# First attention's scores: six bf16 products of three parts replaced by three fp32r products of two 12-bit parts, two heads at a time

## The reference

```python
# 16 heads of 16 channels; l = 2048; b = 2
q, k, v = proj(q_w), proj(k_w), proj(v_w)                  # [b, h, l, 16]
scores = einsum('bhid,bhjd->bhij', q, k) / sqrt(16)
scores = scores - abs(j - i) * slope[h]                    # alibi
attn   = softmax(where(j <= i, scores, -inf), axis=-1)     # causal
out    = einsum('bhij,bhjd->bhid', attn, v) @ o_w
# then: layer norm, a spectral product (one folded 256x256 matrix), layer norm,
# a channel attention, layer norm, 8 experts of 1024 hidden units, layer norm
```

## Time and profile before

| | |
|---|---|
| median of 3 runs | 1443.59 us (1443.12 to 1444.44) |
| profiled execution, time | 1443.52 us |
| profiled execution, span of the trace | 1441.7 us |
| granted TensorE clock, mean over the span | 0.978 |
| PE, DVE, ACT, POOL busy | 1387.3, 1071.8, 869.8, 257.9 us |
| front | 0 to about 907 us |
| maxima reduces L1798 | 576, 643.7 us busy |
| exponentials L1610 | 1120, 585.1 us busy |
| score matmuls L1216 and L1243 | 5120 each |

### The profile page before, as it was taken

How to read it: one execution, slowest core, us unless ns; L and a number is a source line. 1 busy time by engine, 2 the same in 40 slices (tenths; PEclk the granted TensorE clock), 3 DMA queues, 4 the chain that set the end, 5 groups by cost and what they waited for, 6 DMA issues and landing times. The chain is left out here.

```text
span 1441.7 us, 44126 instructions
## 1 busy us (share of the span) xinstructions
PE 1387.3 (96%) x18460; PEld 864.1 (60%) x18460; DVE 1071.8 (74%) x2004; ACT 869.8 (60%) x1775; POOL 257.9 (18%) x388
## 2 busy tenths in 40 slices
PE   7999999999999999999999999899987799999998
PEld 4554444444444444444444445788776689999997
DVE  2666888888888888888888880555788577767666
ACT  3445758788787787787777877655455233333342
POOL 4322111102110111021111110000356401111111
PEclk9999999999999999999999999999997599999999
DMA  7674511112212211122300000314424544454441
GB/s 220 201 176 137 91 33 38 44 30 51 46 32 47 44 36 45 31 50 46 92 3 3 3 3 2 116 43 164 165 84 143 195 180 161 174 183 181 175 181 73
DMA packets 77824, 134.08 MB, mean 93 GB/s; under 512 B 12226, under 2 KB 64443, under 8 KB 72252
## 3 DMA queue, kind: packets, MB, share of 16 engines
q1 hardware_dynamic: 59612, 108.84, 25.5%
q10 hardware_dynamic: 14608, 14.00, 3.0%
q0 software_dynamic: 3408, 8.43, 1.6%
HBM read 67.75 MB, written 23.11 MB: 63 GB/s over the span
## 5 line engine op out<-in xcount | busy, mean ns | idle before, releaser
L1798 DVE TENSOR_REDUCE part_max<-pair 128x2 f32<-128x1024 f32 (+2 forms) x576 | 643.7, 1161 | 82.2 <-PE pair L1216 44.7
L1610 ACT ACTIVATE big<-pair 128x512 f32<-128x512 f32 (+1 forms) x1120 | 585.1, 600 | 194.7 <-PE pair L1243 185.4
L1216 PE MATMUL pair<-big 128*32 128x512 bf16 (+3 forms) x5120 | 350.2, 348 | 2.4 <-DVE part_max L1798 2.2
L1243 PE MATMUL pair<-big 128*32 128x512 bf16 (+3 forms) x5120 | 342.1, 349 | 4.2 <-DMA big<-max_t 3.1
L1265 PE MATMUL pair<-big 128*17 128x512 f32 (+3 forms) x2560 | 288.2, 528 | 0.4 <-POOL big L2227 0.3
L1216 PEld LDWEIGHTS pair<-big 128*32 128x32 bf16 x5120 | 128.1, 96 | 179.8 <-DVE part_max L1798 83.0
L1243 PEld LDWEIGHTS pair<-big 128*32 128x32 bf16 x5120 | 126.4, 96 | 154.0 <-ACT big L1610 70.2
L1623 ACT ACTIVATE std<-moments,eps_col 128x1 f32<-128x1 f32 (+1 forms) x110 | 32.5, 295 | 218.7 <-DVE moments L1836 207.1
L1501 PE MATMUL pair<-big,tok 128*128 128x128 f32 x1248 | 148.3, 278 | 10.4 <-DVE big L2111 10.4
L1501 PEld LDWEIGHTS pair<-big,tok 128*128 128x128 f32 x1248 | 147.0, 194 | 13.8 <-DVE big L2111 12.1
L1513 PE MATMUL pair<-big 128*128 x624 | 141.0, 379 | 0.0
(11 more groups left out here) (184 smaller groups left out, 1310.6 us busy)
## 6 DMA issues: line engine op xcount, KB each, us to landing
tok<-big SPq DMA_DIRECT2D x39, 1024.0 KB
big<-in_L_ffn_w SPq DMA_DIRECT2D x16, 1024.0 KB
big<-split_dram SPq DMA_DIRECT2D x216, 64.0 KB, 2.8
split_dram<-big ACTq DMA_DIRECT2D x32, 384.0 KB, 4.1
big<-split_dram SPq DMA_DIRECT2D x42, 256.0 KB, 4.2
big<-routed_dram SPq DMA_DIRECT2D x39, 129.0 KB, 2.1
tok<-in_L_attn_x SPq DMA_DIRECT2D x8, 512.0 KB, 5.8
big<-in_c_query_rows SPq DMA_DIRECT2D x8, 512.0 KB, 4.7
```

The lines of the kernel that those rows point to most:

```text
L1216: mm = pe.matmul(bank[q:q + STRIPE, o:o + w], m.q_op[slot][:, step.qt, h, step.r * P + q:step.r * P + q + STRIPE], m.k_op[slot][:, h, step ...
L1243: mm = pe.matmul(m.bank[step.bank][k:k + STRIPE, n * w:(n + 1) * w], m.k_op[slot][:, h, step.kb * P + k:step.kb * P + k + STRIPE], m.q_op[ ...
L1610: act.activation(m.p_ring[:, step.place, step.heads[0]:step.heads[-1] + 1, step.at:step.at + w], m.bank[step.bank][:, 0:len(step.heads) * ...
L1798: dve.tensor_reduce(m.part_max[(step.u * QT + step.qt) % 2][:, step.r, step.heads[0]:step.heads[0] + n, step.c], banks[:, :, 0:w], X, ALU. ...
```

## The change

- Projected queries and keys are split into **two** parts: the high part is the fp32 number with its low 12 bits cleared, the low part the rest, both kept as fp32. ScalarE copies the product out (`High`), VectorE clears the bits (`Middle`), GpSimd subtracts in place. The store writes two fp32 arrays in place of three bf16 arrays.
- The products are three in place of six: (high, high), (high, low), (low, high), 48 rows; 5 extra rows for alibi and maxima make 53, and 4 more rows, used on diagonal blocks alone, carry part of the mask there. The operands have type fp32r, a form of fp32 that TensorE multiplies in one pass.
- Two heads lie in the two halves of the partitions (rows 0 to 63 and 64 to 127, "lanes"). A product is one matmul with 128 stationary columns on 53 or 57 rows, and the matmuls of two heads use the two halves of the array's rows. The mask of the maxima pass comes from two bf16 matmuls for each lane.
- `Weigh` is unchanged, but up to two key blocks are taken in one step. The last diagonal block's scores take two exponentials of two heads in place of one of four.
- The constants for the operands are first copied from DRAM to DRAM on ScalarE's queue, and SP waits for that; loads of one unit are 32 in place of 31, of the fixed rows 8 in place of 4.
- The planner's booked costs are remade: it keeps a clock for each lane, books 220 and 130 for going from lanes to the whole array and back, and prefers other steps to `Weigh` when an engine behind would run dry.

```diff
-TERMS = [(0, 0), (0, 1), (0, 2), (1, 0), (1, 1), (2, 0)]
+TERMS = [(0, 0), (0, 1), (1, 0)]
-EXTRA = 32
+EXTRA = 5
+DEEP = EXTRA + len(TERMS) * HD
@@ planner
+    SWITCH = {(True, False): 220, (False, True): 130}
+    def whole(self, cost):
+        self.pe = max(self.pe, *self.lanes) + self.SWITCH.get((self.split, False), 0) + cost
+        self.lanes, self.split = [self.pe] * LANES, False
+    def on_lane(self, lane, cost):
+        self.pe = max(self.pe + self.SWITCH.get((self.split, True), 0), self.lanes[lane])
+        self.lanes[lane], self.split = self.pe + cost, True
+        return self.lanes[lane]
...
@@ weigh
+        while self.to_weigh and len(blocks) < 2 and ... and self.to_weigh[0][-1] <= self.pe:
+            blocks.append(self.to_weigh.pop(0))
@@ step
+        if name == "weigh" and others and (self.act < self.pe + 1200 or self.dve < self.pe + 1600):
+            ...
@@ Chunk, TensorE
-                for q in range(0, P, STRIPE):
-                    mm = pe.matmul(bank[q:q + STRIPE, o:o + w],
-                                   m.q_op[slot][:, step.qt, h, step.r * P + q:step.r * P + q + STRIPE],
-                                   m.k_op[slot][:, h, step.c * TILE:step.c * TILE + w], start=True, ...)
+            for n in range(step.per_bank):
+                for lane in range(LANES):
+                    rows = lane_rows(lane, step.c == step.qt)
+                    mm = pe.matmul(banks[lane][:, n * w:(n + 1) * w],
+                                   m.q_op[slot][rows, step.qt, ..., step.r * P:(step.r + 1) * P],
+                                   m.k_op[slot][rows, ..., step.c * TILE:step.c * TILE + w], ...)
@@ Score, TensorE
-                for k in range(0, P, STRIPE):
-                    mm = pe.matmul(m.bank[step.bank][k:k + STRIPE, n * w:(n + 1) * w],
-                                   m.k_op[slot][:, h, step.kb * P + k:step.kb * P + k + STRIPE],
-                                   m.q_op[slot][:, step.qt, h, step.q0:TILE], start=True, ...)
+                mm = pe.matmul(m.bank[step.bank][:, n * w:(n + 1) * w],
+                               m.k_op[slot][rows, h // LANES, step.kb * P:(step.kb + 1) * P],
+                               m.q_op[slot][rows, step.qt, h // LANES, step.q0:TILE], start=True, ...)
@@ Middle, VectorE (High and its scalar_tensor_tensor are gone)
+            dve.tensor_scalar(m.parts[step.slot][:, 0, :].bitcast(I32), m.parts[step.slot][:, 1, :].bitcast(I32),
+                              -(1 << LOW_BITS), None, ALU.bitwise_and).then_inc(s.high, 1)
@@ start, SP
+    sp.wait_ge(s.rows_out, 16 * (2 + GROUPS))
     first_rows(sp, m, s, 0, s.first_in[0])
```

## The result

The changed kernel takes **1472.4 us** (median of four runs, 1467.6 to 1481.4) against 1443.9 us for the kernel before on the same chip: a ratio of 1.0203, 95% interval 1.0160 to 1.0246. It is 2% slower; 1365 us was forecast. The profiled execution took 1481.4 us, the longest of the four, 9 us over the median. Its front ends (start of the last turn of the sums) at 946 us in place of 906, and what follows takes some 534 us in place of 535: the whole difference lies in the front.

A forecast was written before the change was run, and what follows sets the result against it. TensorE was taken to bound the front, busy 707 of 712 steady us, with VectorE next. Savings of 66 (steady), 9 (mixed) and 4 (tail), 79 us, from 1443.5 gave 1365 us; own range 1325 to 1395, stated range 1320 to 1445.

The forecast's parts named there:

- A pair every 0.215 us: Score products: two heads' 512-column products run at once in both lanes at the bf16 rate, 0.215 us for two heads.
- 234 us saved in both passes: TensorE's scores in the front: 468 us for both passes would fall to 234 us.
- I take nothing: Weight loads of the score products: hidden beside matmuls, cost nothing; could cost up to 243 us.
- the load rule: Rival on score weight loads: they overlap matmuls only on other row groups; 0.19 us exposed each, 1512 us; chance 10%.
- Rate by bytes: Rival on score products: four-byte elements enter at half rate, scores stay 468 us, 1514 us in all; chance 10%.
- Going between lanes and whole array: TensorE's round trips around each weighing: 0.25 us each, 160 to 320 more trips, 60 us taken.
- is no longer the bound: TensorE in the steady stretch of the front: 575 us of work, below VectorE's 606.
- 16 to 96 us: VectorE in the steady stretch: late chunks over 160 to 320 weigh steps, 0.1 to 0.3 us each.
- I take 40: VectorE's late starts in the steady stretch: 40 us on 606 of work, 646 in place of 712, 66 less.
- two engines in step: Rival in the front: VectorE stays at 87% share, fixed order with two rooms can't hide TensorE's steps; 1420 us; chance 18%.
- a clock below 1.00: Sign of a wrong forecast: granted TensorE clock below 1.00 in the front; no size given.
- Mixed stretch and tail: Front's stretch mixing projections and chunks: 9 us less; tail after the last chunk: 4 us less, between 0 and 7.

The follow-up runs named there:

- e1_pairs: Changed kernel with the planner holding a score step back until banks for both lanes are free, then issuing both: 1487.4 us, 1.0289 of the kernel before.
- e5_free: Changed kernel with VectorE's reduces and ScalarE's exponentials both handling only 64 columns of each head, TensorE's order kept: 1361.4 us (one run).
- e6_free_vector: Changed kernel with only VectorE's reduces cut to 64 columns of each head: 1459.6 us (one run).
- e7_free_scalar: Changed kernel with only ScalarE's exponentials cut to 64 columns of each head: 1431.2 us (one run).
- e8_replan: Changed kernel, instructions kept, with the planner's booked costs and thresholds chosen anew, one block a weigh step: 1418.9 us, 0.9835 of the kernel before.
- e9_old_rows66: Kernel before with its score products reading 66 of the 128 rows, nothing else changed: 1444.3 us (one run).

## Why the prediction was wrong

**Scores.** *A pair every 0.215 us* was right for a pair whose load is hidden (0.23 measured). *234 us saved in both passes* was not: it took every product to have its partner in the other lane. They stream for 135 + 187 = 322 us in place of 234. By their own records 909 of the 2560 products overlap with none in the other lane and 1186 with less than half their length; the 1068 of the forecast for e1_pairs lies between. Another 179 us pass with no lane at work; 216 trips of 0.31 make 67 at most of it, as part of each trip is counted with the weighing. The array is held for 936 us, where 715 us of work had been forecast, and with both neighbours freed (e5_free) it still needs some 820 (6.5 to 826).

**Weight loads.** *I take nothing* was right only for products that follow others closely: at 0.23 us a pair leaves no room for a load of 0.19 in the open, and the load rule that I had weighed as a rival (the Trainium skill, "TensorE: Matmul & The Clock Gate", The mechanism, in Part 3) does not hold in those rows, where loads lie beside matmuls of both lanes. But where a load starts with its product, the product takes 0.11 us longer. Away from the slow stretches that happens at 444 starts behind another operation, partly counted in the trips, and at 424 within the lanes, often behind a wait for a bank that the load waits out too. The latter come to some 45 us, an estimate (424 x 0.105) for a term that the sum had at nothing; no run takes it away alone. **Rate by bytes** is excluded: even the pair of 0.34 us lies below the 0.37 from which on it would decide.

**Going between lanes and whole array.** 0.25 us taken, 0.31 measured, 216 steps inside the 160 to 320: 67 us for 60.

**VectorE**, the step that failed: TensorE *is no longer the bound*, and then *16 to 96 us* of late starts, *I take 40*. Of the 116 us between the forecast and the profiled execution 96 lie in the steady stretch, 742 us in place of 646. Its granted clock of 0.95 makes 742 x 2 x 0.05 = 74 us at the lower level, at 0.41 some 30 us. Of the other 712 VectorE works for 621 (620.74, 621.22 before): the 15 us by which I had shortened the reduces did not come (1220 ns each, as in the earlier trace rows). **It stands for 91 us in place of 40**, near my own upper end of 96 and no less than before (there, too, 712 less 621): the gain of 66 us was not there. I had reckoned a late start as one trip and half a chunk, with the array always ready to refill. It was not: no lane streams for 179 us, for 179 and 177 us when one neighbour is freed (e6_free_vector, e7_free_scalar), and for 112 when both are. That is the rival *two engines in step*, and its condition was met at full clock (88.4% against 87.5%). Its price, 1420 us, was not: it took 606 us of work in place of 621, left out the clock, and kept the 9 us of the mixed stretch, which did not come. e8_replan, at 1419, shows what the order withheld; that it hits this number is no proof of the rival's sum.

The Trainium skill ("TensorEngine Tiling (Array Packing)", PSUM Bottleneck) says that tiling speeds TensorE up but not the emptying of PSUM, which may then set the pace. Here the trace agrees, with e5_free's 120 us beside it.

**Clock**, missing from the sum. I named a clock below 1.00 as a sign of error and gave it no price and no chance. By the estimate above it is worth some 35 us in the profiled execution (27 in the median run) and makes the difference between no gain (911 against 906 us for the front) and 2% slower.

**Mixed stretch and tail.** 9 us less were expected of the mixed stretch, and nothing came: 44 reduces in 110 us, at a clock of 0.95, where 45 took 112. The tail was to be 41 us and is 54: after the last chunk ScalarE has 80 instructions and 38.3 us of work left where it had 70 and 33.8.

**Start, queues, DMAs.** Nothing was expected, and 1.4 us were lost: the first operand load goes out 6.7 us later than before, and the first chunk at 39.75 waits 2.76 us for it. Kernel after, start:

```profile
28.67 0.33 SPq L2421 DMA_DIRECT2D k_op<-split_dram  x1
...
39.75 0.62 PE L1259 MATMUL pair<-k_op,q_op 57*128 57x128 f32 x4 [2.76 <-DMA q_op<-split_dram]
```

The bit clearing, taken at 0.69 us, cost 0.43:

```profile
L1816 DVE TENSOR_SCALAR big<-big 128x512 int32<-128x512 int32 x32 | 13.8, 431 | 44.4 <-ACT big L1643 44.4
```

## What to carry to other kernels

When the busiest engine is made twice as fast, its neighbours do not take the time over by themselves: in a fixed order with two or three buffers, count for each step which engine's buffer it needs, and price the standing before it, not only the engines' sums. The written order has to be chosen again for the new durations, and a control with the old instructions and an order chosen anew belongs beside it (8 of 25 us here). And a busy share made of overlapping records says little; the spacing of starts against the columns streamed shows the pauses, and the start of a load against the start of its matmul shows which loads are in the open.

## What the hardware showed that I had not expected

- TensorE's granted clock fell to 0.50 for 16 stretches, 85 us together, in a front whose records show it 96% busy. Before twelve of them were a few microseconds of products, many on one lane, with little weighing between, before the first four longer pauses. The Trainium skill ("TensorE: Matmul & The Clock Gate", A second HAM failure mode: psum-queue depth-cycling) tells of a kernel whose short pauses at PSUM banks send the clock back and forth; this trace agrees in kind, with those 16 stretches, and in e5_free, where the banks are empty sooner, 2 are left (14 us). But the kernel before has pauses of 0.53 and 0.67 us at PSUM banks, with no weighing between, and no fall, where e9_old_rows66 on 66 rows has the same pauses and a fall; so pauses are not shown to be the only cause.
- Two 53-row fp32r products of 512 columns in the two halves of the rows start every 0.23 us together when their weight loads of 0.19 us lie beside the pair before, and every 0.34 us when the loads start with them.
- The effects of freeing two engines did not add up: 18 and 46 us alone, 120 together in the end of the front.
